# Column halves, spread casts and row loads from Pool in layers 2 and 3 of a graph network

## The reference

```python
h = jnp.maximum(_layernorm(x, axis=-1), 0.0)
xn = _bn(h, g0, be0)
h = _bn(relu(_gcn_conv(xn, src, dst, ew, W1, b1, n)), g1, be1)             # 128 -> 256
h = _bn(relu(_graph_conv(h, src, dst, ew, Wrel2, brel2, Wroot2, n)), g2, be2)  # 256 -> 256
h = _bn(relu(_graph_conv(h, src, dst, ew, Wrel3, brel3, Wroot3, n)), g3, be3)  # 256 -> 128
out = x + h

def _graph_conv(x, src, dst, ew, Wrel, brel, Wroot, n):
    agg = segment_sum(ew[:, None] * x[src], dst, num_segments=n)
    return agg @ Wrel + brel + x @ Wroot
```

## Time and profile before

| | |
|---|---|
| median of 3 runs | 3771.5 us (3755.3 to 3779.79) |
| profiled execution | 3759.16 us, its span 3757.3 us |
| granted TensorE clock over the span | 0.883 |
| PE busy | 2988.7 us (80%) |
| DVE busy | 2613.1 us (70%) |
| ACT busy | 2327.1 us (62%) |
| POOL busy | 1348.4 us (36%) |
| layer 2, first dense product to last chunk's products | 1339 to about 2437 us |
| layer 3 | 2480 to 3218 us |
| output | 3242 to 3757 us |

### The profile page before, as it was taken

One profiled execution on the slowest core, in us unless ns is written; L12 is line 12 of the kernel. 1 busy time (PEld: TensorE's weight loads), 2 busy tenths in 40 slices (PEclk: granted clock), 3 DMA queues, 4 the chain that ended last, 5 costly groups with the idle time before them and its releaser, 6 DMA issues. The chain is left out here.

```text
span 3757.3 us, 52409 instructions
## 1 busy us (share of the span) xinstructions
PE 2988.7 (80%) x12445; PEld 2000.6 (53%) x12445; DVE 2613.1 (70%) x5586; ACT 2327.1 (62%) x4070; POOL 1348.4 (36%) x1194
## 2 busy tenths in 40 slices
PE   3565658988899769999999999959999999554543
PEld 3455534444444346777777777735555555333332
DVE  6576647877777858888888888757877777533332
ACT  4586736666666547877788778736666666333331
POOL 1444555545455232222222221022222321067475
PEclk9787879999999979999999999979999999655555
DMA  5586648888788769999999999769999999799997
GB/s 202 192 286 223 228 169 298 309 294 299 287 313 306 273 215 345 337 340 339 343 334 340 346 340 339 275 208 320 346 348 351 346 339 339 290 368 362 378 361 233
DMA packets 344639, 1142.11 MB, mean 304 GB/s; under 512 B 55625, under 2 KB 103266, under 8 KB 294386
## 3 DMA queue, kind: packets, MB, share of 16 engines
q1 hardware_dynamic: 221468, 933.98, 66.6%
q0 software_dynamic: 62656, 77.70, 12.2%
q10 hardware_dynamic: 60438, 129.60, 9.7%
HBM read 625.81 MB, written 515.28 MB: 304 GB/s over the span
## 5 line engine op out<-in xcount | busy, mean ns | idle before, releaser
L1170 POOL DMA_INDIRECT l_ed_gathered<-agg_rows,pos_cols x392 | 432.0, 1102 | 1462.7 <-PE l_ps L1182 704.0
L1078 DVE TENSOR_TENSOR l_dn_hi<-l_dn_hi,l_dn_top 128x512 fp32r<-128x512 f32 x784 | 501.5, 687 | 248.2 <-ACT l_dn_top L1050 228.0
L1023 PE MATMUL l_ps<-l_dn_top,wroot_top 128*128 128x512 f32 x1176 | 503.0, 428 | 85.9 <-ACT l_dn_ho L1037 43.3
L1037 ACT ACTIVATE l_dn_ho<-l_ps,bias_fold 128x512 f32<-128x512 f32 x588 | 395.8, 682 | 151.9 <-PE l_ps L1023 148.6
L1050 ACT ACTIVATE l_dn_top<-l_dn_hi 128x512 fp32r<-128x512 f32 x784 | 448.0, 623 | 65.2 <-DMA l_dn_hi<-h_dense 65.2
L1023 PE MATMUL l_ps<-l_dn_hi,wroot_top 128*128 128x512 f32 x1176 | 466.8, 397 | 0.0
L1023 PE MATMUL l_ps<-l_dn_top,wroot_rest 128*128 128x512 f32 x1176 | 466.4, 397 | 0.0
L685 PE MATMUL l_ps<-l_dn_columns,w_fold 128*128 128x512 f32 x784 | 391.3, 624 | 62.5 <-ACT l_dn_ho L720 55.6
L1608 POOL DMA_INDIRECT out<-out_rows_dst,out_cols x196 | 305.2, 1557 | 289.5 <-DMA out<-out_od_ot 189.6
L609 PE MATMUL norm_ln_ps<-norm_ln_ho 128*128 128x130 f32 x1568 | 248.3, 319 | 182.9 <-ACT norm_ln_ho L597 93.3
L597 ACT ACTIVATE norm_ln_ho<-norm_ln_x,norm_ln_nbias,norm_ln_rstd 128x128 f32<-128x128 f32 x784 | 303.8, 480 | 106.5 <-DVE norm_ln_nbias L550 102.8
(11 more groups left out here) (233 smaller groups left out, 5900.2 us busy)
## 6 DMA issues: line engine op xcount, KB each, us to landing
h_dense<-l_dn_ho SPq DMA_DIRECT2D x196, 1024.0 KB, 10.2
l_dn_hi<-h_dense SPq DMA_DIRECT2D x196, 1024.0 KB
l_dn_rows<-h_rows SPq DMA_DIRECT2D x98, 520.0 KB
h_rows<-norm_ln_ho SPq DMA_DIRECT2D x97, 520.0 KB
h_dst<-l_ed_ho SPq DMA_DIRECT2D x98, 512.0 KB, 10.6
l_ed_hd<-h_dst ACTq DMA_DIRECT2D x98, 512.0 KB
h_dense<-l_dn_ho SPq DMA_DIRECT2D x98, 512.0 KB
out_od_hi<-h_dense SPq DMA_DIRECT2D x98, 512.0 KB
```

The costliest lines, as they stand in the source:

```text
L1023: ins = pe.matmul(o, a, b, start=t == 0, stop=t == len(terms) - 1)
L1037: act.activation(ho[:, j, m, c * CW:(c + 1) * CW], ps[:, u % 2, 0:CW], ACT.Relu, bias=bf[:, m:m + 1]).then_inc(rl[j], 1)
L1078: dve.tensor_tensor(rest[:, j, k, cc], hi[:, j, k, cc], top[:, j % 2, k, cc].bitcast(FP), ALU.subtract).then_inc(spl[j], 1)
L1170: pool.indirect_dma_start(tg[:, j, g, :], None, tab[n - 1][:, :], bass.IndirectOffsetOnAxis(ap=pos_c[:, t:t + 1], axis=0)).then_inc(gat[j] ...
```

## The change

It has three parts. The columns of a dense tile's units change places with the output halves: units now go through both output halves of column half 0 and then those of column half 1. The casts of a tile are spread: one stands behind each relu of layer 2 (two behind each in layer 3), those of column half 0 at lag 8 and those of column half 1 a turn later, at lag 9; DVE's rests follow them. The tops of destination rows in layer 2 are cast by DVE and not by ACT. The loads of flags and weights are issued by POOL, those of chunk k-2 behind the gathers of chunk k, where ACT issued them before.

```diff
@@ tensor, relu and statistics of dense_layer
-                        m, c = divmod(u, CH)
+                        c, m = divmod(u, mb)
@@ scalar of dense_layer
-                def tops(c):
-                    def cast(i, j):
-                        if c == 0:
+                def cast(c, k):
+                    def top_of(i, j):
+                        if c == 0 and k == 0:
                             wait_use(act, got[j], i, 16)
                         i2, j2 = before(i, j, 2, NS)
-                        wait_use(act, mm[j2], i2, per, per - CH + c + 1)
-                        for k in range(kb):
-                            cc = slice(c * CW, (c + 1) * CW)
-                            act.activation(top[:, j % 2, k, cc], hi[:, j, k, cc], ACT.Copy).then_inc(tp[j], 1)
+                        wait_use(act, mm[j2], i2, per, (c + 1) * mb)
+                        cc = slice(c * CW, (c + 1) * CW)
+                        act.activation(top[:, j % 2, k, cc], hi[:, j, k, cc], ACT.Copy).then_inc(tp[j], 1)
...
+                casts = [(late + c, cast(c, k)) for c in (1, 0) for k in range(kb)] if split else []
                 stages = []
                 for u in range(per):
                     stages.append((ahead, relu(u)))
-                    if split and u >= per - CH:
-                        stages.append((late, tops(u - per + CH)))
+                    stages += casts[u * len(casts) // per:(u + 1) * len(casts) // per]
@@ vector of dense_layer
-                return NS, [(ahead + 1, statistics)] + ([(late, rests)] if split else []), end
+                return NS, [(ahead + 1, statistics)] + ([(late + 1, rests(1)), (late, rests(0))] if split else []), end
@@ gpsimd of edge_layer
+                def load_rows(k):
+                    i, j = divmod(k, slots)
+                    wait_use(pool, scn[j], i - 1, kb)
+                    pool.sem_inc(gate_l, 1)
+                    pool.dma_start(ss[:, j, :], line(r_same, k)).then_inc(in_b[j], 16)
+                    if n == 2:
+                        pool.dma_start(cf[:, j, :], line(r_ew, k)).then_inc(in_b[j], 16)
+
                 def end():
+                    for k in range(slots):
+                        load_rows(k)
                     for k in range(EC):
...
+                        if k >= 2 * slots:
+                            load_rows(k - slots)
+                    for k in range(EC - slots, EC):
+                        load_rows(k)
@@ scalar of edge_layer
-                    load_rows(i, j)
@@ the stages one turn ahead, layer 2
-                def hd_rest(i, j):
+                def hd_parts(i, j):
+                    i1, j1 = before(i, j, 1, slots)
+                    wait_use(dve, in_c[j], i, 32)
+                    wait_use(dve, mm_d[j1], i1, mb)
+                    for k in range(kb):
+                        dve.tensor_copy(d_top[:, k, :], hd_in[:, j, k, :]).then_inc(d_tp[j], 1)
                     for k in range(kb):
                         wait_use(dve, d_tp[j], i, kb, k + 1)
                         dve.tensor_tensor(d_rest[:, j, k, :], hd_in[:, j, k, :], d_top[:, k, :].bitcast(FP), ALU.subtract).then_inc(d_rs[j], 1)
```

More of the change, by code:

```diff
@@ L1071, in end, with rests, half @@
                         dve.wait_ge(st[j], per * uses(NS, j))
-                def rests(i, j):
-                    for c in range(CH):
+                def rests(c):
+                    def half(i, j):
                         for k in range(kb):
@@ L1078, in rests @@
                             dve.tensor_tensor(rest[:, j, k, cc], hi[:, j, k, cc], top[:, j % 2, k, cc].bitcast(FP), ALU.subtract).then_inc(spl[j], 1)
-                return NS, [(ahead + 1, statistics)] + ([(late, rests)] if split else []), end
+                    return half
+                return NS, [(ahead + 1, statistics)] + ([(late + 1, rests(1)), (late, rests(0))] if split else []), end
             work = dict(sync=sync, tensor=tensor, scalar=scalar, vector=vector, late=late)
@@ L1347, in load_source @@
                         act.dma_start(inv[:, j, :], line(r_isrc, k)).then_inc(in_a[j], 16)
-                def load_rows(i, j):
-                    k = i * slots + j
-                    act.dma_start(ss[:, j, :], line(r_same, k)).then_inc(in_b[j], 16)
-                    if n == 2:
-                        act.dma_start(cf[:, j, :], line(r_ew, k)).then_inc(in_b[j], 16)
                 def load_dst(i, j):
@@ L1428, in hd_rest @@
                         dve.tensor_tensor(d_rest[:, j, k, :], hd_in[:, j, k, :], d_top[:, k, :].bitcast(FP), ALU.subtract).then_inc(d_rs[j], 1)
-                return slots, [(l_dst - 1, hd_rest)], None
-            def scalar_parts(act):
-                def hd_top(i, j):
-                    i1, j1 = before(i, j, 1, slots)
-                    wait_use(act, in_c[j], i, 32)
-                    wait_use(act, mm_d[j1], i1, mb)
-                    for k in range(kb):
-                        act.activation(d_top[:, k, :], hd_in[:, j, k, :], ACT.Copy).then_inc(d_tp[j], 1)
-                return slots, [(l_dst - 1, hd_top)], None
+                return slots, [(l_dst - 1, hd_parts)], None
             work = dict(sync=sync, gpsimd=gpsimd, tensor=tensor, vector=vector, scalar=scalar)
-            return (work, dict(vector=vector_parts, scalar=scalar_parts)) if n == 2 else work
+            return (work, dict(vector=vector_parts)) if n == 2 else work
         def fold(ph, n, blocks, groups, weight, folded, b_in, b_out, ps=None):
```

2 lines of the change are left out of this document (1 added, 1 removed).

## The result

The change made the kernel slower by 3.4%: 3896.03 us in the median of 4 runs (3881.62 to 3899.9) against 3763.4 us of the kernel before on the same chip (3752.23 to 3779.79). The ratio is 1.034, 95% interval 1.030 to 1.038. The forecast was 3706 us and faster.

The account below looks back on a forecast made before the run. PE was taken to bound layer 2, with one 1.11 us hole a round from ACT's order. 50 + 8 + 7 = 65 us off the 3757.3 us span gave 3692.3; plus 1.9 and 12.3, 3706 us, range 3685 to 3760.

Parts of the forecast that it names:

- The hole in layer 2: Steady layer 2: PE waits 1.11 us a round for a relu behind ACT's casts; closing it gains 50 us.
- Layer 3 unchanged at 99% PE: Sign expected in layer 3: PE stays busy at 99%, with no gain or loss there.
- so they meet no wait: ACT's first casts of a turn, column half 1 of the tile before: their tops' buffer is already freed.
- no such hole: Layer 3 before the change: PE busy 99.67 us of 100, and ACT waits for PE.
- Beginnings: Starts of layers 2 and 3: earlier weights and flags from POOL gain 8 and 7 us, bounds 0 and 17.
- DVE's casts at 0.43 us each, no cost: Layer 2: two destination casts add 0.86 us a round to DVE, covered by PE's chunk work; cost zero.
- POOL's loads, taken at 1.4 us each: Row loads issued by POOL: 1.4 us each, between bounds 0.34 and 1.40, fitting POOL's idle 16.1 us a round.
- Earlier by up to a round: Steady part: POOL's row loads come up to a round earlier, worth nothing since nobody waited.
- The rival that transfers bind: Layer 2: transfers become the bound, giving 3739 us at 344 GB/s or 3757 at 338; chance 0.13.
- The slower rival: Layer 2: DVE waits for destination rows and stops PE, 3824 us if loads land at 16.5 us; chance 0.09.

Follow-up runs that it names:

- dense part alone: Kernel before plus new unit order, spread casts, and half 1's casts and rests at lag 9; destination casts and row loads stay on ACT: 3908.08 us, 1.040.
- late rests only: Kernel before with one edit: DVE makes the rests of column half 1 at lag 9 instead of 8, ACT's casts unmoved: 3834.97 us, 1.020.
- spread with the lead kept: The changed kernel with all casts and rests of both column halves at lag 8, unit order and spread casts kept: 3748.73 us, 0.986.
- edge parts again: Kernel before plus destination casts on DVE and row loads from POOL, dense tiles as before, second measurement: 3752.76 us, 0.987.
- product waits by half: The changed kernel, but PE waits for each column half's rests ahead of that half's units, not once for all four: 3624.7 us, 0.999.
- both ideas: The changed kernel with PE's wait split by column half and layer 3's casts ahead of the relu of their place: 3654.52 us, 1.007.

## Why the prediction was wrong, point by point

- *The hole in layer 2, 45 x 1.11 = 50 us: right in place and size.* The round was forecast at 20.84 and is 20.82 us; PE waits nowhere from 1500 to 2300 us. ACT's casts in a row are confirmed as the cause of the hole, but the prediction credited the spread casts and the moved ones together (a backlog of 0.52 us for 2.08) and didn't ask which was needed. The hole closes (20.9 us) with the destination casts alone. The dense part alone leaves 21.2.
- *"Layer 3 unchanged at 99% PE": the step that failed, +144.5 us.* The prediction asked of the casts at lag 9 only whether they would have to wait ("so they meet no wait") and not who waits for them. The rests moved from two turns ahead of the product to one. In layer 3 a turn is 2.8 us of PE's dense work, while affine, relu, casts and rests take 3.9 us (2917.60 to 2921.54), and ACT begins with them only 1.2 us after PE has begun its tile (2916.39). The sum costed layer 3's dense part at zero without naming cover; the row of layer 3 with PE at 99.67 was read as "no such hole", when it also said that nothing is spare there. About 41 of the 144.5 us fall at the beginning: from layer 3's first dense product to the eleventh chunk's transposes it takes 174 us, where it took 134.
- *Beginnings: gain forecast 15 us, layer 2's beginning lost about 37.* POOL's loads alone gave 9 us of medians. DVE's waits for weights and flags (1.41, 7.67 and 6.99 us in the earlier trace rows) are gone from both beginnings, so their mechanism holds and the size was too large. POOL's first gathers, which come behind the loads, were not free either: PE waited for them for 1.6 us in layer 2 and 0.7 us in layer 3, and for 2.8 us in layer 2 with the loads moved alone, where the kernel before has no such wait. The loss is the lag again, in the turns without a dense tile, and the run with late rests only shows it without any other part.
- *DVE's casts at 0.43 us each, no cost: right.* The group of 98:

```profile
L1438 DVE CAST l_ed_hd_top<-l_ed_hd 128x512 fp32r<-128x512 f32 x98 | 37.0, 420 | 0.0
```

  DVE is busy for 91 of 100 us in layer 2 (forecast 92), and PE waits once for `l_ed_sum_rest`, 0.5 us.
- *POOL's loads, taken at 1.4 us each: too dear, without effect on the sum.* One is 0.59 us. "Earlier by up to a round" in the steady part is wrong for layer 3, as the run with the loads alone shows.

```profile
2902.97 0.59 POOL L1168 DMA_DIRECT2D l_ed_same<-row_same  x1
```

- *The rival that transfers bind: it did not come.* From 1500 to 2300 us layer 2 moves 357 GB/s at a share of 1.00, where it moved 340 before, and PE waits for nothing; single stretches of 100 us reach 354 and 366. The Trainium skill (HBM Reference, Specifications) gives about 358 GB/s as a core's share. The mean is what the new round asks for (356 by the prediction), so it doesn't tell that figure from a higher one; only the stretch at 366 and the 387 of the output lie above it.
- *The slower rival was the wrong one.* DVE didn't wait for the destination rows (no such wait is listed for the beginning of layer 2, and none stops PE in the steady part). The case that came, a lost lead in layer 3, had no chance of its own, though the part on the change said that half 1's casts come a turn later.

Settled by runs: the lag of half 1 is the whole loss, its rests act at the beginnings, casts and rests together in steady layer 3, and it acts through PE's single wait ahead of a tile (with that wait split, the round falls from 17.2 to 15.1 us). Open: what exactly decides whether the clock falls after a wait of 1.9 us.

## What to carry to other kernels

When a stage moves to a later turn, count the distance to its consumer in the shortest turn of any phase that runs the same code, and again where items go at half rate; asking only whether the moved stage itself waits misses it. If work is split in halves so that it can come later, the consumer's wait has to be split the same way, or the second half's lateness is paid by the first. And try the parts of a change apart: here two casts moved to an engine that had room for them (DVE, at 84 of 100 us) gave all of the gain (1.3%), and the elaborate part gave nothing measurable beyond it, and the loss.

## What the runs showed of the hardware

- A plain load issued by POOL took 0.59 us of POOL's time, between ACT's 0.34 us and a gather's 0.95 to 1.67 in the rows shown.
- DVE made the cast of 128x512 in 420 ns in the mean of 98, where ACT needs 520 ns from one cast to the next. With POOL's loads beside it or without (destination casts alone) the median is the same, 421 and 422 ns.
- PE's clock in layer 3: after 1.86 us of idling the granted clock was 0.57 for the next 4 us, after another 1.92 us it stayed at 1.00. In the mean a round lost 2.4 us for 1.9 us of waits.
- The stages ahead of layer 2, which the change doesn't touch, are not the same in every set of runs. Busy times at the start of the kernel before, and of the kernel with the destination casts alone, up to just behind the beginning of layer 1:

```profile
0.00:510.00 510.00, 258.47 (x1611) 236.07 (x1612) 303.55 (x1875) 307.87 (x789) 213.04 (x233) 0.81 0.63 217
```

```profile
0.00:403.00 403.00, 214.41 (x1619) 193.73 (x1620) 303.59 (x1881) 306.62 (x790) 212.65 (x233) 0.95 0.80 274
```

  DVE and ACT are busy for the same time; the clock and the transfer rate are not the same. The work on the layer norm's input tile spans 420 us in the first (42.2 to 462.3) and 311 us in the second (42.1 to 352.9). It isn't the chip by itself: four of the traces come from chips numbered 10, and it is 426 us in the earlier two (spread with the lead kept, edge parts again) and 312 us in the later two (product waits by half, both ideas). Layer 1 varies as well, from its first product to layer 2's first dense product 842, 804, 882 and 817 us (kernel before, casts alone, lead kept, waits by half). What decides is open. The steady rounds of layer 2 and 3 agree to 0.1 us between all sets. This is where the kernel before gets medians from 3627 to 3809 us here, and why each ratio is taken within one set.
